# Finer steps for the weaving of one instruction order: a kernel of two transformer-like layers on one core

## What is computed

```
x = x + layernorm(x) @ (weight * block_mask).T                      # block 1
x = x + layernorm(x) @ (int4 nibbles * scale).T + bias              # block 2
x = x + block3(layernorm(x))                                        # block 3: all weights are NF4 codes
x = x + block4(layernorm(x))                                        # block 4: NVFP4 rounding of x, of the weights, of h
# block 3: W = NF4[codes] * scale (64 wide blocks), each product with a LoRA part beside it
#   attn = (q + k + v) / 3 ; x1 = z + o(attn) ; h = silu(g(x1)) * u(x1) ; out = x1 + down(h)
```

## Time and profile before

| | |
|---|---|
| median of 3 runs | 782.47 us (779.07 to 785.65) |
| the profiled execution | 782.3 us, span of its trace 780.7 us |
| PE busy | 703.8 us, mean granted clock 0.969 |
| DVE, ACT, POOL busy | 545.1, 448.0, 219.7 us |
| loads and norms, blocks 1 and 2 | 0 to 141 us |
| merge and o | 141 to 200 us |
| gate, up, down with the NF4 decoding | 200 to 450 us |
| rest of them, then block 4 | 450 to 780 us |

### The profile page before, as it was taken

One profiled execution on the slowest core, in us unless ns is written; L12 is line 12 of the kernel. 1 busy time (PEld: TensorE's weight loads), 2 busy tenths in 40 slices (PEclk: granted clock), 3 DMA queues, 4 the chain that ended last, 5 costly groups with the idle time before them and its releaser, 6 DMA issues.

```text
span 780.7 us, 10709 instructions
## 1 busy us (share of the span) xinstructions
PE 703.8 (90%) x3830; PEld 528.6 (68%) x3830; DVE 545.1 (70%) x1017; ACT 448.0 (57%) x582; POOL 219.7 (28%) x208
## 2 busy tenths in 40 slices
PE   2799866797999989999998999997999999989998
PEld 1566533575777756677675777775777789967886
DVE  6889886656577677878798976587543534487883
ACT  3767778476778596887886712374332111245552
POOL 1004100003355547557578554220401000000000
PEclk9999977898999999999999999999999999989999
DMA  9646588887457677686875301210301111100001
GB/s 339 191 142 210 159 248 252 258 283 223 175 164 242 190 244 251 210 258 204 263 220 185 122 28 37 69 52 18 107 28 38 30 35 36 56 1 13 28 28 40
DMA packets 55540, 110.78 MB, mean 142 GB/s; under 512 B 9904, under 2 KB 20560, under 8 KB 55232
## 3 DMA queue, kind: packets, MB, share of 16 engines
q1 hardware_dynamic: 42912, 80.28, 32.7%
q0 software_dynamic: 4384, 14.09, 6.2%
q10 hardware_dynamic: 8192, 15.73, 6.0%
HBM read 92.19 MB, written 17.89 MB: 141 GB/s over the span
## 4 chain that ended last, share of the span: by engine, by line
PE 56%; DVE 16%; ACT 8%; DMA 8%; issue 7%; SPq 4%; ACTq 0%; POOL 0%; DVEq 0%; POOLq 0%
PE bank L1287 15%; PE bank L1288 14%; PE bank L1289 14%; DMA rep<-codes 4%; ACT hot L1709 3%; PE bank L1401 2%; DVE hot L1958 2%; DMA wide_buf<-in_down_flat 2%; DVE x L2071 1%; PE bank L1596 1%; PE bank L1443 1%; ACT c L1666 1%; DVE bank L1984 1%; PE bank L1547 1%; DVE q_a L2034 1%
## 5 line engine op out<-in xcount | busy, mean ns | idle before, releaser
L1709 ACT ACTIVATE hot<-rep,levels 128x2048 f16<-128x2048 f16 x94 | 192.9, 2092 | 25.6 <-DMA rep<-codes 15.4
L1287 PE MATMUL bank<-zt_h,w_h 128*128 128x512 f32 (+1 forms) x232 | 93.5, 403 | 2.5 <-DVE zt_l L2059 2.0
L1288 PE MATMUL bank<-zt_l,w_h 128*128 128x512 f32 (+1 forms) x232 | 91.6, 395 | 0.0
L1289 PE MATMUL bank<-zt_h,w_l 128*128 128x512 f32 (+1 forms) x232 | 91.5, 394 | 0.0
L1287 PE MATMUL bank<-w_h,xq_h 128*128 128x512 f32 (+1 forms) x192 | 73.9, 385 | 2.3 <-ACT xq_l L1803 2.1
L1289 PE MATMUL bank<-w_h,xq_l 128*128 128x512 f32 (+1 forms) x192 | 71.7, 373 | 0.0
L1288 PE MATMUL bank<-w_l,xq_h 128*128 128x512 f32 (+1 forms) x192 | 71.7, 373 | 0.0
L1401 PE MATMUL bank<-hot,diag 128*32 128x512 f16 x856 | 60.6, 394 | 8.6 <-ACT hot L1709 8.2
L1958 DVE TENSOR_SCALAR hot<-rep,levels 128x2048 f16<-128x2048 f16 x56 | 52.7, 941 | 7.1 <-DMA rep<-codes 7.0
L1996 DVE TENSOR_TENSOR w_l<-bank,w_h 128x512 fp32r<-128x512 f32 x46 | 31.7, 689 | 35.9 <-ACT w_h L1717 35.6
L2214 POOL TENSOR_TENSOR q_a<-q_a,q_m 128x384 f32<-128x384 f32 (+3 forms) x34 | 35.9, 1055 | 65.6 <-DVE q_m L1845 65.5
(11 more groups left out here) (215 smaller groups left out, 1666.2 us busy)
## 6 DMA issues: line engine op xcount, KB each, us to landing
rep<-codes SPq DMA_DIRECT2D x56, 512.0 KB, 4.8
codes<-c SPq DMA_DIRECT2D x28, 256.0 KB, 3.6
raw<-in_codes_gu_t ACTq DMA_DIRECT2D x14, 512.0 KB, 5.7
sc<-in_scales_gu_t SPq DMA_DIRECT2D x56, 128.0 KB, 3.9
raw<-in_codes_attn_t ACTq DMA_DIRECT2D x7, 512.0 KB, 5.0
raw<-in_codes_down_t ACTq DMA_DIRECT2D x7, 512.0 KB, 5.8
sc<-in_scales_down_t SPq DMA_DIRECT2D x28, 128.0 KB, 3.1
wide_buf<-in_gate_flat SPq DMA_DIRECT2D x5, 512.0 KB, 4.7
```

The lines of the kernel that those rows point to most:

```text
L1287: PE.matmul(psum, lh, rh, start=first, stop=False, **kw)
L1288: PE.matmul(psum, lh, rl, start=False, stop=False, **kw)
L1289: return PE.matmul(psum, ll, rh, start=False, stop=last, **kw)
L1709: S.activation(hots[plan.slot[hot_ring(t), (t, m)]][:], codes_in_place(t), ACT.Relu, bias=levels[:, at:at + 1], scale=levels[:, at + 1:at ...
```

## The change

The norm-and-product step of `stages()` becomes two steps, with a yield after the norm's part and one after the product's, and `known` moves behind the second, so that it stands one part after its `var`. (`norm` calls `known` itself where it has not come yet; before, that was so for the second half of each norm, and after the change it never comes to that.) The NF4 tile takes three steps: the look step without hits, then hits(t+1), then assemble(t), scales(t+3) and, for even t, cast and fetch. The rates are scaled with it, so that tiles per main step are as before (0.6 x 0.5 = 0.3; 1.4 x 3/2 x 1/2 = 1.05; 1.0 x 3/2 = 1.5; 0.86 x 3/2 = 1.29). Both orders have the same 1698 steps, and so the same instructions.

```diff
-INT4_RATE = 0.6
-EARLY_RATE = 1.4
-ATT_RATE = 1.0
-NF4_RATE = 0.86
+INT4_RATE = 0.3
+EARLY_RATE = 1.05
+ATT_RATE = 1.5
+NF4_RATE = 1.29
...
         fetch(2)
+        yield
         hits(0)
...
             high_parts()
-            if u == 0 and i + 2 < len(jobs):
-                cast(i + 2)
-                if i + 3 < len(jobs):
-                    fetch(i + 3)
             if u == 1 and i + 2 < len(jobs):
                 ship(i + 2)
...
             low_parts()
+            yield
             if t + 1 < tiles:
                 hits(t + 1)
...
                 assemble(t)
                 scales(t + 3)
+            if u == 0 and i + 2 < len(jobs):
+                cast(i + 2)
+                if i + 3 < len(jobs):
+                    fetch(i + 3)
             yield
...
             for n in norm_turn(ln):
-                if added and added[1] % HN == HN - 1:
-                    known(added[0], added[1] // HN)
+                yield
                 if turned and turned[0]:
...
                 yield
+                if added and added[1] % HN == HN - 1:
+                    known(added[0], added[1] // HN)
...
-    side_max = Side(greatest, MAX_RATE / 2)
+    side_max = Side(greatest, MAX_RATE / 3)
```

## The result

The changed kernel takes **808.57 us** (median of 3 runs, 808.2 to 811.9) against 782.47 us: ratio 1.037, 95% interval 1.032 to 1.042. The forecast was 784.0 us with a range of 771 to 796, so the result lies outside it, on the side of rival 2 and well beyond its 792. The profiled execution took 808.57 us itself, with a span of 807.3 us; that of before had 780.7 us, so there are 26.6 us to account for.

A forecast was written before the change was run, and what follows sets the result against it. PE's work was taken as fixed, with ACT's queue order setting its idle time. From 782.3 us, -5.0 up to the merge, 0 in attention and +6.6 in the loop gave 783.9, forecast 784.0 us, range 771 to 796.

The forecast's parts named there:

- rival 2: Gate/up/down loop: ramps behind the silu, alone, make it slower; ramp waits above 13 us, 792 us; chance 0.28.
- What bounds the kernel: Whole kernel: PE's work stays the same; the change moves only its idle time, about 77 us, and time at the lower clock.
- part 2: Way to the merge, 104 to 141 us: no gain of its own, 0.5 us lost; a merge at 141 or later would refute it.
- Part 1: Blocks 1 and 2, 20 to about 104 us: -3.5 us in block 1, about -0.5 us in block 2.
- the reciprocals: Third norm: assemble(11) now stands behind them on DVE, so ACT's 3.12 us wait shortens: -1.5 us.
- the walk: Stepping through the engines' queues with measured durations; for the loop's old order it gave 4.2 us of ramp waits against 8.2 measured.
- the DMA crowding: Before the merge: fetch, stored codes and spread issued within about 1 us may delay rep 17, and the merge by 2 us.
- The sentence on the clock: Before the merge, 110 to 141 us: PE still has nothing to multiply, so the low-clock cost stays where it is.
- Attention: Attention keeps its order but for casts behind ramps, where ACT was idle before and after: 0, within 1 us.
- Part 3: Gate, up and down with decoding, 200 to 450 us: ramp waits about 16.5 us against 8.2; +6.6 us, bounds -6 and +13.
- (a) to (c): Loop: cast no longer ahead of odd ramps; ramps behind silus, 4 x 1.3 us; close looks wait 0.7 to 3.3 us.
- Rival 1: Whole kernel: smaller portions help everywhere; early -6, ramp waits down by 3: 773 us, chance 0.22.

The follow-up runs named there:

- e1: The changed kernel with hits(t+1) put back into the look step, still three steps a tile: 790.97 us, ratio 1.013.
- e13: The early-only kernel (new order to tile 15, old order after) with hits up to tile 16 one step behind their look: 781.0 us, ratio 0.997.
- e7: The changed kernel with hits back in the look step up to tile 15, and the order and rates of before from tile 16: 775.34 us, ratio 0.991.
- e11: The changed kernel with only ACT's ramps back in the look step, DVE's planes one step later: 792.55 us, ratio 1.013.
- e10: The changed kernel with only DVE's planes back in the look step, ACT's ramps one step later: 808.75 us, ratio 1.036.
- e8: The changed kernel with hits and cast both in their old places, still three steps a tile: 783.53 us, ratio 1.004.
- e2: The changed kernel with cast and fetch back at the head of the look step, hits still a step late: 795.84 us, ratio 1.021.
- e4: The changed kernel with the norm and product step in one part and known as before, NF4 in three steps: 811.15 us, ratio 1.039.
- e5: The kernel before, two steps a tile, with only cast and fetch moved to the end of the tile's second step: 788.17 us, ratio 1.008.
- e12: The early-only kernel (new order to tile 15, old after) with hits ahead of the low parts from tile 16: 775.06 us, ratio 0.993.

## Why the prediction was wrong

**What bounds the kernel, and that PE's work is the same**: right for the instructions (x3830 in both). The sentence that the change can only add idle time and time at the lower clock was right too, but no term of the sum carried the clock. Its own signs came out split: the waits of looks for ramps were forecast at 13 to 17 us in some 12 waits and came as 14.1 in 12, and the merge came at 143.4 us, where it had named 141 or later as the sign against part 2.

**Part 1, -4.0 us, and -1.5 for the reciprocals: the waits right, the sum wrong.** The local waits came as worked out. The waits for tsplit behind late casts in block 2 (2.3 to 3.1 us each) stand beside casts at 73.31, 88.31 and 104.02 us:

```profile
75.55 0.50 PE L1453 MATMUL bank<-zt_h,minus 128*128 128x512 f32 x1 [2.81 <-ACT zt_h L1690]
...
90.53 0.79 PE L1453 MATMUL bank<-zt_h,minus 128*128 128x512 f32 x1 [2.74 <-ACT zt_h L1690]
...
106.30 0.49 PE L1453 MATMUL bank<-zt_h,minus 128*128 128x512 f32 x1 [3.34 <-ACT zt_h L1690]
```

The third norm's first turn no longer waits (2.75 us in the earlier trace rows), and ACT's wait for the reciprocals fell from 3.12 to 0.57 us:

```profile
110.57 0.81 ACT L1683 ACTIVATE ztok<-x,mv,inv_dev 128x512 f32<-128x512 f32 x1 [0.57 <-DVE mv L1910]
```

But the gain that they should add up to is not there. The third norm's first tile (forecast 4.0 us earlier) is scaled at 96.44 us against 97.55, and its fifth (forecast 5.5 us earlier) at 110.57 against 110.26. With hits in their old place (e1) these two stand at 93.92 and 105.38, 3.6 and 4.9 us earlier than before: the walk came near for an order that leaves hits alone, and late hits, which it gave no price in this part but the first look's 0.5 to 0.9 us, ate the rest.

**Part 2, the sum of -5.0 us up to the merge: wrong.** The merge came at 143.43, not at about 136. The step that failed is "By the walk the cast ends when ship(9) was issued before (128.7)". It ended 4.0 us later:

```profile
131.62 1.05 ACT L1669 CAST c<-raw 128x1024 f16<-128x1024 int32 x1
132.69 0.38 SPq L2339 DMA_DIRECT2D codes<-c  x1
133.18 0.55 SPq L2347 DMA_DIRECT2D rep<-codes  x1
139.79 2.09 ACT L1712 ACTIVATE hot<-rep,levels 128x2048 f16<-128x2048 f16 x1 [1.57 <-DMA rep<-codes]
```

The load of rep 17 went out at 133.18 instead of 129.32 and was used at 139.79 instead of 137.28, 2.5 us later, and so the merge is 2.5 us later. The load itself took 6.6 us and not 8, so the DMA crowding that the forecast feared is not the cause. Hits' place is: with hits back the merge is at 136.53 (e1), with late hits and nothing else different at 143.93 (e13 against e7's 136.42). By halves it is the ramps again: 138.46 us with ramps early (e11), 144.62 us with DVE's planes early (e10). One way for late hits to do it stands in the kernel, and was not isolated: SP issues spread(t) only when the planes of tile t-2 are done, since there are two rep buffers. The -5.0 would have been nearly right (-4.4 us) for an order that moves the cast and leaves hits alone.

The sentence on the clock failed too, "Since PE still has nothing to multiply before the merge in the new order, both rule and rows leave this cost where it is". PE's idle time up to the merge fell by 2.6 us, and by 3.6 if one takes out that PE's first matmul came 1.0 us later (13.3 against 12.3 us; how much of that is scatter, two profiles don't say). But the same 634 matmuls took 5.1 us more: from 120 to 140 us the clock is 0.60 and then 0.50, where it was 0.84 before. Whether the low clock helped to make the merge late or only went with it, no run separates.

**Attention, 0 within 1**: -2.0 us, the clock of the merge's neighbourhood (0.93 to 0.97).

**Part 3, +6.6 us: the right place, wrong in size by 18 us.** The step that failed is the list of what the change does there, (a) to (c): it prices the ramps' place, books the cast's place as a gain and has no cost for the third step. By the stretches above the three cost 8.2, 7.5 and 8.1 us. That the first is near the walk's own 8.3 is partly luck, since the walk had no clock and no wait for h in it. The tiles of the walk against the waits of looks in the changed kernel, each tile's waits summed:

| tile | forecast | measured |
|---|---|---|
| 26, 32, 39 | 1.3 each | 0.93, 1.32, 1.56 |
| 46 | 1.3 | 4.01 |
| 34 | 2.7 | 2.21 |
| 38 | 0.8 | 1.49 |
| 40 | none | 2.37 |
| 41 and 42 | 2.1 | 2.50 |
| 44 | 1.5 | 1.06 |
| 48 | 0.7 | 0 |
| 53 and 54 | 3.3 | 5.92 |
| 33, 37 | gone | 0 |
| sum with tile 35 | 16.3 | 23.6 |

The cast's place ahead of odd ramps did go (tiles 33 and 37, 0.80 and 1.59 us before, 0 after). The walk (16.3 us by its own items, not 16.5) is 7.3 us short, and tiles 40, 46, 53 and 54 alone are 7.7 us above it: the ramps of 40, 46 and 53 stand behind an at_h that keeps ACT idle for 4.0, 6.5 and 5.5 us. Inside the walk three terms failed:

- "Smaller portions for DVE should shorten that [...]: I take 1.7 off". The wait grew instead, from 23.0 to 28.8 us over the same work. The portions as such are not to blame: e8 has the same ones and 21.9 us from 200 to 450 us, against 26.4 in the earlier trace rows. What matters is what stands behind the wait. Before, no gu_mul stood between a look and the ramps behind it; the new order puts one there for 8 tiles (8 in e2, e4 and e10 as well, none in e1, e8 and e11). The walk gave ACT durations and no waits.
- DVE's planes had no price. They are 9.5 of the 23.6 us by name, but e10 shows that taking them away brings nothing (808.75 us): the ramps' waits are then 17.7 us.
- The clock had no price either: 9.4 us on the 1200 matmuls of 228 to 446.5 us.

The identical work from 228 us took 15.1 us more idle and 9.4 us more busy time, against +6.6.

**The late cast**, which I had on the gain side only, "the cast no longer stands ahead of odd ramps", costs 0.8% by itself (e5) and up to 1.6% in the changed order. What shows with it in the traces is ACT waiting for rep loads (17.7 us in e1 against 10.2 in e8 with the cast back, 8.1 in the changed kernel against 1.6 in e2, 11.2 in e5 against 8.3 before): a later cast means a later store of the codes and a later load. I had given this path half a microsecond, before the merge, and nothing behind it. That this wait carries the loss of the late cast was not isolated, and e5 speaks against it as the whole: its looks wait less than before. A high part one cast later is the other candidate. The cause stays open; what the runs show is the size.

**The rivals.** Rival 2, the slower one, had a mechanism that is there ("the ramps behind the silu, alone") and the right point of decision (waits for ramps above 13 us: 14.1 came, and e11 against e10 shows the ramps' share), but not the "alone": the ramps' place is some 8 of the 24 us of the loop. What it priced at +12 -2 came as +24.5 and +2.5 -2.0. Rival 1's "the portions help everywhere" is refuted by e8 in the loop, 8.1 us longer, and borne out by it up to the first addition, 4.9 us earlier. The chances (slower by over 1%: 0.28) were too low because the loop's extra idle time, 15.1 us, was more than even the upper bound of +13, and the clock came on top.

## What to carry to other kernels

In one written-out order for all engines, what stands ahead of a producer on its engine counts for more than how fine the steps are. Before moving a step behind another one, list for its in-order engine not only the busy instructions now ahead of it but each of their waits, and follow those waits to the engine and DMA that end them. Price a late TensorE twice, as idle time and as the stretch at the low clock behind it: here 15.1 and 9.4 us. And try the parts of a change by stretch, even where the whole is level: the finer steps with hits in their old place were worth 0.9% up to the merge (e7) and cost 15.6 us behind the first down addition (e1).

## What was not expected of the hardware

The clock's share. In the stretch of 228 to 446.5 us an extra 15.1 us of idle time, in waits of at most 2.5 us, came with 9.4 us of slower matmuls. The two do not stand in a fixed ratio: in the stretch of the last table e5 has 1.7 us more idle time than before and 4.4 us more busy time, e2 6.4 and 3.1. Up to the merge the matmuls became 5.1 us slower although PE's idle time fell. The early orders with the merge at 136.4 to 137.4 us (e1, e5, e7, e12) have 96.9 to 98.3 us of busy time for the same 634 matmuls, and the four with it at 143.4 to 145.7 us (the changed kernel, e4, e10, e13) have 100.9 to 102.3 us. Which order of waits keeps the clock up was not tried by itself.
